# Splitting the last stage's weights in chunks during attention, and issuing the first scores one group earlier

## What is computed

```python
def attn(x, W_qkv, W_out):                       # x: 8 x 512 x 256, normed
    qu, ku, vu, qc, kc, vc = split(x @ W_qkv.T)  # each b, h=8, 512, d=64
    term1 = where(causal_mask, 0.0, (qc * SCALE) @ vu.T)
    lookahead = where(causal_mask, sigmoid((qu * SCALE) @ ku.T), 0.0)
    Su = term1 @ lookahead.T
    scores = where(causal_mask, neg, (qc * SCALE) @ kc.T - silu(Su))
    return heads(softmax(scores) @ vc) @ W_out.T
def ffn(x, w_gate, w_up, w_down):                # int32 weights times 1/127
    return (silu(x @ wg.T) * (x @ wu.T)) @ wd.T
out = x + attn(layernorm(x)) + ffn(layernorm(x))
```

## Time and profile before

| | us |
|---|---|
| median of the runs | 1144.9 |
| the profiled execution, device time | 1145.9 |
| its span, first to last instruction | 1144.2 |
| steps 2 to 30 | about 28.2 each, 29.1 where q = 2 |
| last stage from its first matmul on | 948 to 1144 |

### The profile page before, as it was taken

One profiled execution on the slowest core, in us unless ns is written; L12 is line 12 of the kernel. 1 busy time (PEld: TensorE's weight loads), 2 busy tenths in 40 slices (PEclk: granted clock), 3 DMA queues, 4 the chain that ended last, 5 costly groups with the idle time before them and its releaser, 6 DMA issues.

```text
span 1144.2 us, 21233 instructions
## 1 busy us (share of the span) xinstructions
PE 1092.3 (95%) x7936; PEld 992.5 (87%) x7936; DVE 815.2 (71%) x1671; ACT 763.5 (67%) x1371; POOL 534.2 (47%) x623
## 2 busy tenths in 40 slices
PE   5899999999999999999999999999999859999997
PEld 4799999999898899998999899999999757888997
DVE  5577677777777777777777777777667777567665
ACT  4577777777777777777777777777777846344333
POOL 0255556455645564555455555555555554231130
PEclk9999999999999999999999999999999969999999
DMA  8000201020002000200020012001100403745641
GB/s 284 1 2 19 75 22 22 17 77 22 22 17 76 24 25 13 80 21 20 17 76 20 19 24 70 20 19 39 37 20 19 157 19 130 274 149 176 224 152 57
DMA packets 36952, 73.22 MB, mean 64 GB/s; under 512 B 2288, under 2 KB 15856, under 8 KB 34800
## 3 DMA queue, kind: packets, MB, share of 16 engines
q1 hardware_dynamic: 36848, 71.84, 20.0%
HBM read 42.47 MB, written 32.24 MB: 65 GB/s over the span
## 4 chain that ended last, share of the span: by engine, by line
PE 87%; DVE 7%; issue 2%; ACT 1%; DMA 1%; DVEq 0%; POOL 0%; SPq 0%; ACTq 0%
PE X L637 23%; PE X L561 20%; PE X L675 8%; PE X L752 7%; PE X L743 6%; PE X L591 6%; PE X L646 6%; PE X L605 4%; PE X L576 4%; DVE prob L1147 3%; PE X L621 2%; DMA v_s<-heads_out 1%; PE X L552 1%; DVE low_max L1106 0%; DVE L_s L1200 0%
## 5 line engine op out<-in xcount | busy, mean ns | idle before, releaser
L637 PE MATMUL X<-L_s,T_s 128*128 128x128 f32 (+3 forms) x1920 | 278.9, 303 | 10.0 <-DVE L_s L1119 10.0
L487 POOL TENSOR_SCALAR prob<-prob,inv 128x512 f32<-128x512 f32 (+3 forms) x256 | 278.0, 1103 | 17.1 <-DVE inv L1159 17.1
L637 PEld LDWEIGHTS X<-L_s,T_s 128*128 128x128 f32 x1920 | 267.0, 191 | 20.5 <-issue 10.1
L561 PE MATMUL X<-xT,W 128*128 128x512 f32 x960 | 237.5, 400 | 8.5 <-DVE least L1147 7.0
L561 PEld LDWEIGHTS X<-xT,W 128*128 128x128 f32 x960 | 178.8, 191 | 50.4 <-DVE least L1147 9.7
L900 ACT ACTIVATE gate<-X 128x1024 f32<-128x1024 f32 (+1 forms) x96 | 84.8, 883 | 130.1 <-PE X L637 130.1
L1147 DVE CUSTOM_DVE_ANT_0 prob<-X,gate 128x512 f32<-128x512 f32 (+3 forms) x256 | 109.9, 485 | 73.8 <-PE X L621 73.7
L1133 DVE SCALAR_TENSOR_TENSOR gate<-gate,X 128x1024 f32<-128x1024 f32 (+1 forms) x96 | 99.6, 1038 | 77.9 <-ACT gate L900 77.9
L908 ACT ACTIVATE prob<-prob,least 128x512 f32<-128x512 f32 (+3 forms) x256 | 141.2, 562 | 8.5 <-DVE least L1147 8.5
L477 POOL TENSOR_SCALAR_AFFINE_SELECT T_s<-T_s 128x512 fp32r<-128x512 f32 x128 | 111.1, 889 | 67.0 <-DVE T_s L1126 67.0
L469 POOL TENSOR_SCALAR_AFFINE_SELECT tanh_l<-tanh_l 128x256 f32<-128x256 f32 (+1 forms) x96 | 46.2, 497 | 205.6 <-ACT tanh_l L878 205.6
(11 more groups left out here) (82 smaller groups left out, 1816.3 us busy)
## 6 DMA issues: line engine op xcount, KB each, us to landing
heads_out<-o_s SPq DMA_DIRECT2D x64, 256.0 KB, 3.3
xT_copy<-xT SPq DMA_DIRECT2D x8, 1024.0 KB, 7.6
xb<-in_L_attn_x SPq DMA_DIRECT2D x8, 512.0 KB, 5.8
xT<-xT_copy SPq DMA_DIRECT2D x4, 1024.0 KB, 5.2
tanh_l<-in_L_attn_x SPq DMA_DIRECT2D x8, 512.0 KB, 5.4
gate<-heads_out SPq DMA_DIRECT2D x4, 1024.0 KB, 8.0
T_s<-heads_out SPq DMA_DIRECT2D x4, 1024.0 KB, 9.7
L_s<-xT_copy SPq DMA_DIRECT2D x4, 1024.0 KB, 6.2
```

The lines of the kernel that those rows point to most:

```text
L487: last = pool.tensor_scalar(v, v, inv[:, h, w - 1:w], None, ALU.mult)
L561: last = pe.matmul(out, sh.W[:, a, k, cols], xT[:, c, k, :], start=(n == 0), stop=(n == 3 * KD - 1))
L637: last = pe.matmul(both[:, h, at:at + (J + 1) * P], T_s[:, h, a, to:to + P], L_s[:, h, c, WIDE[J + 1]:WIDE[J + 1] + (J + 1) * P], start=(J ...
```

## The change

Two things change, and the diff below is cut to them.

First, the weights. `copy_weights`, the four `high_weights`, `low_weights` and the three `take_low_max` of step 31 go. In their place the four matrices are cut into 22 chunks of 128 x 256 values. In each of the steps 4 to 25, SP loads one chunk (128 KB) into the tile `w_raw`, ScalarE makes its high part and VectorE its low part in `w_parts`, VectorE reduces it (the first 18 chunks, the integer ones), and SP stores both parts (256 KB) to a DRAM tensor `w_split` in the next step. The flag `has_low` is made in steps 22 to 25. In step 31 SP loads the finished parts, twice the bytes of before, straight into place, and TensorE waits for these loads instead of for `w_low`. ScalarE's list at the start of the last stage has one swap: the exponentials of group 1 come before the copy of the output of pair 30.

Second, TensorE's order in a step: Sc 0 comes between L 1 and L 2. `TURNS` gets the same swap of two rows; each kind keeps the banks that it had (Sc 0 banks 4 and 5, L 2 banks 2 and 3).

```diff
-         ... ("L", 1, (0, 1)), ("L", 2, (2, 3)),
-         ("Sc", 0, (4, 5)), ("Sc", 1, (6, 7)), ...
+         ... ("L", 1, (0, 1)), ("Sc", 0, (4, 5)),
+         ("L", 2, (2, 3)), ("Sc", 1, (6, 7)), ...
@@ tensor, step
                 look_ahead(part, b, g, 1)
+                if back1:
+                    scores(part, b, q, g, 0)
                 look_ahead(part, b, g, 2)
                 if back1:
-                    scores(part, b, q, g, 0)
                     scores(part, b, q, g, 1)
@@ tensor, ffn_first
-                pe.wait_ge(w_low, 2)
+                pe.wait_ge(w_loaded[0], 16)
+                pe.wait_ge(w_loaded[1], 16)
@@ sync, step
+                c = g - FIRST_CHUNK
+                if 1 <= c <= CHUNKS:
+                    store_chunk(c - 1)
+                if 0 <= c < CHUNKS:
+                    load_chunk(c)
+                if c == INT_CHUNKS + 1:
+                    sp.wait_ge(low_most_taken, 1)
+                    sp.dma_start(low_row[:, :], low_most[:, :]).then_inc(low_max_gathered, 16)
...
+                    sp.wait_ge(chunk_stored, CHUNKS * 16)
                     for n in range(4):
-                        sp.wait_ge(w_copied[n], 16)
-                        sp.dma_start(placed[n][:, LOW, :].bitcast(F32 if n == 3 else I32), w_copy[n]).then_inc(w_loaded[n], 16)
+                        sp.dma_start(placed[n].bitcast(F32), w_split[n]).then_inc(w_loaded[n], 16)
...
+            def store_chunk(c):
+                n, at = chunk_of(c)
+                sp.wait_ge(w_low, c + 1)
+                sp.sem_inc(ticks, 1)
+                sp.dma_start(w_split[n][:, :, at:at + CHUNK], w_parts[:, :, :].bitcast(F32)).then_inc(chunk_stored, 16)
@@ scalar, step: after high_L(g, 1), before high_proj(g + 1, QU, par)
-                if part == LAST and q == 3:
-                    high_weights(0)
+                if 0 <= g - FIRST_CHUNK < CHUNKS:
+                    high_chunk(g - FIRST_CHUNK)
...
+            def high_chunk(c):
+                act.wait_ge(chunk_loaded, c * 16 + 16)
+                if c > 0:
+                    act.wait_ge(chunk_stored, c * 16)
+                raw = w_raw[:, :].bitcast(F32) if chunk_of(c)[0] == 3 else w_raw[:, :]
+                act.activation(w_parts[:, HIGH, :], raw, ACT.Copy).then_inc(w_high, 1)
@@ vector, step
                 low_L(g, 2)
-                if part == LAST and q == 3:
-                    low_weights(2)
+                if 0 <= g - FIRST_CHUNK < CHUNKS:
+                    low_chunk(g - FIRST_CHUNK)
...
                 if ahead:
                     low_values(g + 2, (q + 1) // 2 % 2, (q + 1) % 2)
+                if 0 <= g - FIRST_CHUNK < INT_CHUNKS:
+                    take_low_max(g - FIRST_CHUNK)
+                if g - FIRST_CHUNK >= INT_CHUNKS:
+                    take_has_low(g - FIRST_CHUNK)
...
                 if back1:
                     low_PT(g - 1, 0)
-                if part == LAST and q == 3:
-                    take_low_max(0)
-                    take_low_max(1)
-                    take_low_max(2)
                 silu_of(g, 2)
```

More of the change, by code:

```diff
@@ L170, with layer @@
 BEFORE = bank_history()
[L173 removed]
+def layer(nc, x, W_qkv, w_gate, w_up, w_down, W_out, w_split, xT_copy, sh, heads_out, out):
     ctx = ExitStack()
@@ L1045, in step @@
                     high_xT(part, b)
-                if part == LAST and q == 3:
-                    high_weights(3)
                 if ahead:
```

93 lines of the change are left out of this document (46 added, 47 removed).

## The result

| | kernel before | changed kernel |
|---|---|---|
| median of 6 runs, us | 1144.86 | 1126.48 |
| lowest and highest, us | 1143.78 to 1145.54 | 1124.01 to 1129.09 |
| profiled execution, device time / span, us | 1145.91 / 1144.2 | 1126.58 / 1124.9 |
| mean granted clock of TensorE | 0.988 | 0.993 |

The ratio of the times is 0.984, with a 95% interval of 0.983 to 0.986: the change gains 18.4 us. The forecast was 1127.0, with a range of 1123.5 to 1132.8. The profiled executions lie 19.3 us apart.

A forecast was written before the change was run, and what follows sets the result against it. TensorE was taken as the bound, busy 1092.3 of 1144.2 us, so only its gaps and slowed work could be won. Terms of 5.4 and 12.5 us, 17.9 off the 1144.9 median, gave 1127.0 us, range 1123.5 to 1132.8.

The forecast's parts named there:

- (a): Step 31, before Su: without the subtractions and ScalarE's first two weight copies, low_L and Su start 4.1 us sooner.
- (b): Step 31, before the drain's scores: without the three reductions the wait is 1.1 us, a gain of 5.06 us.
- (c): Drain: its scores and output run at full clock, 4.8 us instead of 7.8, a gain of 3.0 us.
- (d): From the first gates and ups to the third: the stretch shortens by 0 to 0.6 us, taken as 0.3 us.
- Part one: TensorE's order, Sc 0 before L 2: QU's wait for VectorE goes, 0.20 us in 29 steps, net 5.4 us.
- Part two: Steps 4 to 25: the chunk's added ScalarE and VectorE operations, about 0.4 us each, are covered and cost 0 us.
- Part three: The end, from step 31 through the drain to the third gate and up: (a) to (d), 12.5 us gained.
- 1 (the clock stays up): Shortened gap before Su of step 31: the clock doesn't fall, another 2.45 us gained, 1124.6 us; chance 0.13.
- 2 (the wait moves): Steps 2 to 30: the new order moves QU's wait instead of removing it, 12.5 us only, 1132.4 us; chance 0.13.
- 5 (late loads): The change doesn't do what it says, such as weight loads arriving late; 1140 to 1145 us; chance 0.03.
- Rivals 3: Six q = 1 steps: additions cost, or VectorE's subtraction waits for a whole scaling; 7 us lost, 1134 us; chance 0.06.
- 4: Middle steps: GpSimd loses a whole scaling to each new VectorE operation, TensorE waits, 26 us lost, 1153 us; chance 0.03.

The follow-up runs named there:

- the first run with idle matmuls: The changed kernel with 26 more 512-wide matmuls, results unused, filling the gap before Su of step 31; 1123.61 us, ratio 0.982.

## Why the prediction was right, term by term

All differences are between the two profiled executions.

| term | predicted, us | shown, us | from |
|---|---|---|---|
| Sc 0 before L 2, to QU of step 30 | 5.4 | 8.05 | 883.28 and 875.23 |
| (a) from there to Su of step 31 | 4.1 | 3.86 | 921.24 and 909.33, less 8.05 |
| (b) from there to the drain's scores | 5.06 | 4.63 | 940.49 and 923.95 |
| (c) scores and output of the drain | 3.0 | 3.1 | 7.80 and 4.71 from scores to gate and up |
| (d) to the third gate and up | 0.3 | 0.56 | 5.34 and 4.78 |
| sum there | 17.9 | 20.2 | 953.63 and 933.44 |
| behind it | 0 | -0.9 | span 19.3 shorter |

**Part one was too small a term.** The wait went, as the step said, but the loss per step was 0.23 us in step 30 (0.72 less 0.49) and about 0.27 in the mean, not 0.20: between QU of step 1 and QU of step 30 it is 7.8 us over 29 steps. The step that failed is the choice of the row: I took the 0.55 us of step 0 for the pace without hindrance, and it is 0.49. The clock is not the reason, since it was at 1.00 until 32 us (the same columns as in the windows above):

```profile
30.00:32.00 2.00, 1.10 (x13) 0.77 (x13) 2.00 (x2) 1.77 (x3) 0.50 (x1) 1.00 0.00 0
```

In the run with the first gaps filled, too, the distance is 0.56 us at a clock of 1.00. But the row itself comes right behind a wait of 0.90 us, with its first weight load starting at 31.33 together with its first matmul; in step 30 of the changed kernel the load is 0.12 us ahead. That this makes the 0.06 us is likely and was not tried. The other end of my bound, the mean wait of 0.24, was the better value, and still low; 0.3 us of the 7.8 is one long step in the profile before (from Su of step 17 to that of step 18, 29.29 us where its like take 28.9 to 29.0), and the rest of the difference is open. The kernel with the order alone gained 6.6 us in the medians and 7.8 in its trace, so the size of part one is known to about 1 us.

**Step 1** did what was said. Sc 0 waits 1.93 us there and L 2 comes behind it. 0.2 us are lost, where I had counted 0.4: the changed kernel is 0.47 us ahead at the end of step 0 and 0.28 at QU of step 1. The 0.47 us itself is no term of the change. The first QU ran faster in this execution (6.57 us instead of 7.00), and executions with the same instructions up to there differ by as much: Su of step 0 starts at 41.40 us in the changed kernel and at 42.23 in the one with 26 idle matmuls in step 31.

**Part two** held as it stands. The chunk's operations took 412, 399 and 407 ns, TensorE waits for none of them (no wait of its own is listed in the steps 2 to 30), and on VectorE q = 1 is the thinnest cover, as the run with more subtractions showed.

**Part three.** (a) was right in mechanism: the gap is 6.10 us (5.9 predicted), the clock falls in it, and Su stays slow, 9.85 us against 9.51. That is 0.34 of the 0.67 us that (a) and (b) together fell short. (c) has the right size, 3.1 us, and half of the reason. It took the slow matmuls for what held up the first gate and up. But before the change the flag held it up as well, and at the same moment: in the run with the order alone the output ran at full pace and the gate and up came no sooner behind the drain's scores, 7.80 us in both. The term came out because the change takes both away, the slow clock and the late flag; the second was not in my account, and that the size held was luck. (d) is within its 0 to 0.6 us, but by the run with the copy first the swap alone is worth 0.77 us in this place, so the softmax seems to have brought nothing.

**Behind the third gate and up** I had written that the order is the same, and counted nothing. 0.9 us was given back there: 0.15 in batch 0, where a wait of 0.25 us for the turned probabilities is new; 0.37 at the wait in batch 1, which grew from 0.36 to 0.73 us, because the loads of the output have their own time; and 0.37 behind VectorE's last sum, which is still 19.68 us earlier (1117.97 instead of 1137.65), since the store of the last output landed 5.1 us after its issue instead of 4.8.

The sum came out within 0.5 us partly by luck: part one was 2.2 us too small, and the 0.47 us of the start came on top; (a) and (b) were 0.67 too large and (c) and (d) 0.35 too small; 0.9 us was lost at the end; and the medians lie 0.9 us closer together than the profiled executions.

**Rivals.** 1 (the clock stays up) did not occur; kept up by force it is worth 2.7 us. 2 (the wait moves) is excluded by the trace of the order alone, where TensorE waits once for VectorE in the steps 2 to 30, 0.2 us. 5 (late loads) is excluded by loads that landed some 25 us early. Rivals 3 and 4 would need the chunk's operations and GpSimd's scaling to hold each other up, and the scaling says no: in this kernel it takes 1567 ns in the mean, and 1564 before.

```profile
L518 POOL TENSOR_SCALAR prob<-prob,inv 128x512 f32<-128x512 f32 x28 | 43.6, 1567 | 0.0
```

In step 24 the subtraction runs in the midst of eight scalings, and takes its 0.41 us (in step 4, with a chunk of integers, it is the same at 151.42 us):

```profile
711.86 8.53 POOL L518 TENSOR_SCALAR prob<-prob,inv 128x512 f32<-128x512 f32 x8
713.92 0.71 DVE L1155 SCALAR_TENSOR_TENSOR L_s<-tanh_l,L_s 128x512 fp32r<-128x512 f32 x1 [0.17 <-ACT L_s L926]
714.56 0.41 DVE L1131 TENSOR_TENSOR w_parts<-w_raw,w_parts 128x256 fp32r<-128x256 f32 x1
```

## What to carry to other kernels

Before a row serves as the pace without hindrance, look at what stands in front of it and at the granted clock: a row right behind a wait was 0.06 us too long here, which is 1.7 us over 29 steps. When two limits end at the same moment, the trace names one of them; the other shows only when the first is gone. So when work leaves the critical place of a kernel, list everything that hangs on its result, also a single flag that a branch reads: it can take over as the last wait. And where an engine's list puts something that comes through DRAM ahead of work that doesn't, that place is a fixed point in time, at which a gain in front of it can be given back; move it in the one batch where it is late, since in the others the same order can cost.

## What the runs showed of the hardware

**The same gap can cost the clock or not.** Before the scores of step 1 TensorE was idle for 1.93 us in the changed kernel, and the granted clock stayed at 1.00; in the first run with idle matmuls it was idle there for 1.91 us, and the clock fell, to the lower of its two levels (1.2 instead of 2.4 GHz):

```profile
56.92 1.36 PE L652 MATMUL X<-kc_s,qc_s 64*128 64x512 f32 x6 [1.91 <-DVE T_s L1171]
```

```profile
58.00:60.00 2.00, 2.00 (x19) 1.97 (x16) 1.31 (x4) 1.04 (x2) 0.24 (x2) 0.50 0.01 4
```

So the length of the idle time before a place doesn't tell by itself what the clock does behind it. The Trainium skill, page "TensorE: Matmul & The Clock Gate", section "Part 1: The HAM clock gate (the "warmup" mystery)", says of the start of a kernel that the number of matmuls at the lower clock differs between runs of the same kernel. These two traces agree: their instructions are the same up to step 31, and Su of step 1 starts at 67.33 us in one and at 69.69 in the other. So the start alone can move a run by 2.4 us. Whether this is the scatter of the changed kernel isn't shown: its six runs lay 5 us apart, and the four with the gaps of steps 0, 1 and 31 filled 1.6 us, but the four with the copy first, which fill no gap, lay only 0.6 us apart.

**VectorE beside GpSimd.** `low_L` of group 0 took 1.48 us in this kernel. It now starts while GpSimd still masks `T_s`:

```profile
706.47 1.82 POOL L508 TENSOR_SCALAR_AFFINE_SELECT T_s<-T_s 128x512 fp32r<-128x512 f32 x3
...
707.88 1.48 DVE L1155 SCALAR_TENSOR_TENSOR L_s<-tanh_l,L_s 128x1024 fp32r<-128x1024 f32 x1
...
710.16 1.22 DVE L1155 SCALAR_TENSOR_TENSOR L_s<-tanh_l,L_s 128x1024 fp32r<-128x1024 f32 x1
710.41 1.47 POOL L508 TENSOR_SCALAR_AFFINE_SELECT T_s<-T_s 128x512 fp32r<-128x512 f32 x1 [2.12 <-DVE T_s L1162]
```

The same operation took 1.22 us a little later, when it started before GpSimd's next mask, and then the mask took 1.47 us instead of the 0.6 of the three above. Between 300 and 700 us the mean of the 28 was 1320 ns, and 1242 before. With the order alone it was 1307 ns and with the chunks alone 1243, so it is the order that brings it. It hid behind other work. The Trainium skill, page "SBUF — State Buffer", section "SBUF: two separate sides", says that a VectorE operation with two SBUF inputs and a GpSimd operation that reads SBUF take their shared ports in turn, each for a whole instruction. Both rows fit a wait for the end of the other's instruction, within 0.15 us (spans on GpSimd are rough). So does the row in the last stage of the run with the first gaps filled: GpSimd's sum starts at 965.86 us and takes 1.26, VectorE's low part starts at 965.89 and takes 1.78 instead of 0.67. In the changed kernel the two start in the same instant, at 967.93; there the low part takes 0.67 us, and it is the sum that takes 1.82 instead of 1.29.

The rows of step 24 above don't fit it: there the same kind of operation ran in the midst of scalings at 0.71 us, and the scalings lost nothing. In the run with four more subtractions a little was lost on both sides: the 320-wide subtractions took 477 to 802 ns, and the 384-wide scalings between 150 and 700 us 1367 ns in the mean instead of 1262. By the runs here the rule holds for GpSimd's masks and sums, and not for its scaling beside the operations of the changed kernel; which property decides was not tried.
